# Four sums of the scan stage as accumulating transfers within SBUF, and the forget-gate product behind the B product

## The reference

```python
def step(yt, wx_t):                      # recurrence over 3136 tokens, for 64 images at once
    yt = jax.nn.sigmoid(wx_t + yt @ Vt)
    return (yt, yt)
t = t + ys                               # residual: this is x2
# third part, on xn = ln(x2)
forget_gate = sigmoid(x_ri @ Wf + bf + 2.0); input_gate = sigmoid(x_ri @ Wi + bi)
delta = softplus(x_ri @ Wd + bd) * 0.1
Bx_r = Br * x_r - Bi_ * x_i;   Bx_i = Br * x_i + Bi_ * x_r
inp = delta * input_gate * Bx
def step(h_state, _):                    # 16 steps from zero, per element
    Ah_r = Ar * h_r - Ai * h_i;   Ah_i = Ar * h_i + Ai * h_r
    return ((fg_r * Ah_r + inp_r, fg_i * Ah_i + inp_i), None)
x = x + h                                # this is x3
```

## Time and profile before

| | us |
|---|---|
| median of 3 runs | 13394.81 (13394.42 to 13395.24) |
| the profiled execution | 13372.47 |
| its span | 13370.7 |
| DVE busy | 10838.4 (81%) |
| PE busy | 10073.0 (75%) |
| ACT busy | 9336.7 (70%) |
| POOL busy | 4891.2 (37%) |
| scan stage | from about 5210 to 11715 |

### The profile page before, as it was taken

One profiled execution on the slowest core, in us unless ns is written; L12 is line 12 of the kernel. 1 busy time (PEld: TensorE's weight loads), 2 busy tenths in 40 slices (PEclk: granted clock), 3 DMA queues, 4 the chain that ended last, 5 costly groups with the idle time before them and its releaser, 6 DMA issues. The chain is left out here.

```text
span 13370.7 us, 227528 instructions
## 1 busy us (share of the span) xinstructions
PE 10073.0 (75%) x79508; PEld 7480.1 (56%) x79508; DVE 10838.4 (81%) x22723; ACT 9336.7 (70%) x21751; POOL 4891.2 (37%) x4455
## 2 busy tenths in 40 slices
PE   7888888888888886777777777777777776455544
PEld 5666666666676665555555555555555554123343
DVE  6777777777777773599999999999999999999910
ACT  6888888888888885566767667666666666467710
POOL 4444454444444442112112112112112112178856
PEclk9999999999999997777777777777777777677755
DMA  3333333333333332111121121111211211076544
GB/s 71 79 84 88 84 79 79 80 87 88 79 79 79 84 86 69 32 53 52 48 56 50 49 56 49 52 53 48 56 50 48 57 45 38 17 139 123 105 79 69
DMA packets 1599947, 907.59 MB, mean 68 GB/s; under 512 B 60693, under 2 KB 1537368, under 8 KB 1598820
## 3 DMA queue, kind: packets, MB, share of 16 engines
q1 hardware_dynamic: 1345060, 756.57, 23.7%
q10 hardware_dynamic: 207104, 102.79, 2.7%
q0 software_dynamic: 46656, 33.68, 2.0%
HBM read 567.56 MB, written 325.32 MB: 67 GB/s over the span
## 5 line engine op out<-in xcount | busy, mean ns | idle before, releaser
L1237 PEld LDWEIGHTS s_pW<-s_XU,s_vh 128*128 128x128 f32 x6272 | 1416.1, 261 | 1969.7 <-ACT s_XU L1108 1699.7
L1237 PE MATMUL s_pW<-s_XU,s_vh 128*128 128x64 f32 x6272 | 1492.9, 331 | 1071.6 <-ACT s_XU L1108 1071.6
L1108 ACT ACTIVATE s_XU<-s_pW,s_zb 128x64 f32<-128x64 f32 x3136 | 992.5, 316 | 1790.1 <-PE s_pW L1237 1739.5
L833 POOL TENSOR_TENSOR s_rst<-s_var,s_epst 128x16 f32<-128x16 f32 (+1 forms) x100 | 141.7, 1417 | 3907.2 <-DVE s_var L80 3907.2
L1266 PE MATMUL s_pG<-s_wg,s_XNT 128*128 128x384 f32 (+1 forms) x3200 | 1507.3, 560 | 37.6 <-ACT s_Z L1087 37.6
L409 ACT ACTIVATE KB<-pV,qkb 32x392 f32<-32x392 f32 x2048 | 1189.6, 581 | 25.9 <-PE pV L499 1.9
L249 POOL TENSOR_TENSOR SS<-SS,mx 128x784 f32<-128x784 f32 x512 | 769.5, 1503 | 805.0 <-DVE mx L342 804.8
L1204 PEld LDWEIGHTS s_pY<-s_hident,s_XU 128*128 128x128 f32 (+1 forms) x3200 | 751.7, 305 | 177.7 <-issue 129.5
L257 POOL TENSOR_TENSOR XR<-XR,pbias 112x512 f32<-112x512 f32 x448 | 571.8, 1276 | 648.7 <-DMA XR<-in_x_dram 648.7
L461 ACT ACTIVATE XH<-XR,nm,rs 112x128 f32<-112x128 f32 x1792 | 731.3, 482 | 90.4 <-POOL nm L268 81.8
L507 PE MATMUL pS<-KB,QT 128*64 128x196 f32 x8192 | 793.2, 336 | 0.0
(11 more groups left out here) (262 smaller groups left out, 29675.0 us busy)
## 6 DMA issues: line engine op xcount, KB each, us to landing
XL<-in_x_dram SPq DMA_DIRECT2D x64, 1568.0 KB, 12.4
XR<-in_x_dram SPq DMA_DIRECT2D x64, 1568.0 KB, 18.0
x_dram<-XR SPq DMA_DIRECT2D x64, 1568.0 KB, 8.1
xh_dram<-XH SPq DMA_DIRECT2D x64, 1568.0 KB, 8.1
e_X<-out_dram SPq DMA_DIRECT2D x64, 1568.0 KB, 15.0
s_XQ<-xh_dram ACTq DMA_DIRECT2D x384, 256.0 KB, 2.8
out_dram<-s_IN SPq DMA_DIRECT2D x96, 1024.0 KB, 5.9
e_W<-in_w_dram SPq DMA_DIRECT2D x128, 256.0 KB, 3.2
```

Source lines behind the costliest of these rows:

```text
L1108: act.activation(XU[j % 2][:, t, :], pW[t // R % 2][:, B * (t % R):B * (t % R) + B], ACT.Tanh, bias=zb[:, 0:1], scale=0.5).then_inc(u_sb, 1)
L1237: pe.matmul(pW[t // R % 2][:, B * (t % R):B * (t % R) + B], vh[:], before, start=False, stop=True, skip_group_check=True).then_inc(z_ps, 1)
```

## The change

Four additions are taken from DVE and done by DMAs that POOL issues with `accum_op=ALU.add`, which add one SBUF tile of 1 MB onto another: the two halves of the B product (`Dl` onto `BX`), the two halves of the A product (now `Z` onto `Wv`), and the last two sums (`XN` onto `X2`, then `Wv` onto `X2`). SP stores x3 from `X2` in place of `IN`, and the next load of that buffer waits for the store. The last two products are four operations of half the size, two into `XN` and two into `Wv`. The factor 0.5 and its offset move into the copy of x2, which becomes an activation with a bias of 0.5. The forget-gate product moves behind the B product and three further operations, to place 12 of the chain, and ACT's first gate waits for that.

```diff
-                    sp.wait_ge(dv, o * NV + NV)
-                    sp.dma_start(tokens(x3_d, OS * s_, OS, c),
-                                 IN[0:size(c)].rearrange("t r b c -> t (r b c)").rearrange("t (b c) -> t b c", b=OS)
-                                 ).then_inc(x3_st, 16)
+                    sp.wait_ge(both_added, (o + 1) * 16)
+                    sp.dma_start(tokens(x3_d, OS * s_, OS, c), X2[o % NX][0:size(c)]).then_inc(x3_st, 16)
...
+            def add_state(o):
+
+                n = size(o // NO)
+                pool.wait_ge(dv, o * NV + NV - 2)
+                pool.dma_start(X2[o % NX][0:n].rearrange("t b c -> t (b c)"), XN[0:n].rearrange("t b c -> t (b c)"),
+                               accum_op=ALU.add).then_inc(first_added, 16)
+
+            def add_input(o):
+
+                n = size(o // NO)
+                pool.wait_ge(dv, o * NV + NV)
+                pool.wait_ge(first_added, (o + 1) * 16)
+                pool.dma_start(X2[o % NX][0:n].rearrange("t b c -> t (b c)"),
+                               Wv[0:n].rearrange("t r b c -> t (r b c)"),
+                               accum_op=ALU.add).then_inc(both_added, 16)
...
+                    pool.wait_ge(wp_d, o + 1)
+                    pool.dma_start(Wv[0:tm].rearrange("t r b c -> t (r b c)"), Z[0:tm].rearrange("t r b c -> t (r b c)"),
+                                   accum_op=ALU.add).then_inc(wv_d, 16)
...
+                    pool.wait_ge(bp, oc + 1)
+                    pool.dma_start(BX[0:tc].rearrange("t r b c -> t (r b c)"), Dl[0:tc].rearrange("t r b c -> t (r b c)"),
+                                   accum_op=ALU.add).then_inc(bx_d, 16)
...
-                dve.wait_ge(part_sem, n + 1)
-                dve.tensor_tensor(flat(out[0:tc]), flat(out[0:tc]), flat(Dl[0:tc]), ALU.add).then_inc(sem_, 1)
...
                     after(7)
-                    turned_by(tm, Wv, inp, a, wp_d, wv_d, o)
+                    wait(dve, both_added, o * 16)
+                    turned_by(tm, Wv, Z, inp, a, wp_d)
                     dve.wait_ge(am, o * NA + 3)
                     did(dve.scalar_tensor_tensor(t1, d0, -2.0, t1, ALU.mult, ALU.subtract))
-                    dve.wait_ge(wv_d, o + 1)
-                    did(dve.scalar_tensor_tensor(flat(wv), flat(tf), 1.0, flat(wv), ALU.add, ALU.mult))
...
+                    wait(dve, first_added, o * 16)
                     did(dve.scalar_tensor_tensor(f1[:, 1], t1, -1.0, d1, ALU.add, ALU.mult))
                     did(dve.scalar_tensor_tensor(f0[:, 0], f0[:, 0], -0.25, d0, ALU.add, ALU.add))
+                    dve.wait_ge(wv_d, (o + 1) * 16)
+                    did(dve.scalar_tensor_tensor(flat(wv), flat(tf), 1.0, flat(wv), ALU.add, ALU.mult))
...
-                act.copy(X2[oc % NX][0:tc, Q * q:Q * q + Q, :].rearrange("t b c -> t (b c)"), pY[0:tc, :]).then_inc(x2_d, 1)
+                act.activation(X2[oc % NX][0:tc, Q * q:Q * q + Q, :].rearrange("t b c -> t (b c)"), pY[0:tc, :], ACT.Identity,
+                               bias=cols[0:tc, 1:2]).then_inc(x2_d, 1)
...
                 if i == 0:
-                    wait(act, dv, (oc - 1) * NV + 9)
+                    wait(act, dv, (oc - 1) * NV + 12)
```

More of the change, by code:

```diff
@@ L780, in load_x1 @@
                 c, s = divmod(o, NO)
-                wait(sp, dv, (o - NX + 1) * NV)
+                wait(sp, x3_st, (o - NX + 1) * 16)
                 sp.dma_start(X2[o % NX][0:size(c)], tokens(x1_d, OS * s, OS, c)).then_inc(x2_ld[o % NX], 16)
@@ L814, in _ @@
             pool.tensor_tensor(fld[4], fld[3], nhalf[:, 0:C], ALU.pow).then_inc(pch, 1)
+            def add_state(o):
[10 more added lines that the diff above has]
+                               accum_op=ALU.add).then_inc(both_added, 16)
             for j, s, oc, o, scan, prep in slots():
+                if o is not None and o >= 1:
+                    add_input(o - 1)
                 if scan and s == NO - 2:
@@ L819, in _ @@
                     pool.wait_ge(raw_d, j + 1)
-                    wait(pool, bx_d, (j - 1) * NO)
+                    wait(pool, bp, (j - 1) * NO)
                     pb = par_b[j % 2][0:tj]
@@ L842, in _ @@
                     pool.tensor_tensor(sa[0:tj], sa[0:tj], phalf[0:tj], ALU.pow).then_inc(mag_d, 1)
+                if oc is not None:
+                    tc = size(oc // NO)
+                    pool.wait_ge(bp, oc + 1)
+                    pool.dma_start(BX[0:tc].rearrange("t r b c -> t (r b c)"), Dl[0:tc].rearrange("t r b c -> t (r b c)"),
+                                   accum_op=ALU.add).then_inc(bx_d, 16)
+                if o is not None:
+                    add_state(o)
+            add_input(NGR - 1)
         @block.vector
@@ L898, in rows, with turned_by @@
                 return v.rearrange("t r b c -> t r (b c)")
-            def turned_by(tc, out, of, coef, part_sem, sem_, n):
+            def turned_by(tc, out, part, of, coef, part_sem):
                 def by(first):
@@ L1038, in _ @@
                     after(20)
-                    did(dve.scalar_tensor_tensor(rows(wv), both(f0[:, 0]), 1.0, rows(wv), ALU.add, ALU.mult))
-                    did(dve.scalar_tensor_tensor(rows(inp), both(f0[:, 1]), 1.0, rows(inp), ALU.add, ALU.mult))
+                    for r in range(2):
+                        did(dve.scalar_tensor_tensor(XN[0:tm, :, HC * r:HC * r + HC], f0[:, 0], 1.0, wv[:, r],
+                                                     ALU.add, ALU.mult))
                     after(22)
[L1042 to L1046, removed]
+                    for r in range(2):
+                        did(dve.scalar_tensor_tensor(grouped(wv)[:, :, HC * r:HC * r + HC], f0[:, 1], 1.0, inp[:, r],
+                                                     ALU.add, ALU.mult))
                 if scan and s == NO - 2:
@@ L1119, in _ @@
                             act.wait_ge(rs_d, oc + 1)
-                            wait(act, dv, (oc - 1) * NV)
-                            wait(act, bx_d, oc)
+                            wait(act, first_added, (oc - 1) * 16)
+                            wait(act, bp, oc)
                             wait(act, n_ps, oc * NQ)
@@ L1152, in _ @@
                         if conv:
-                            act.wait_ge(bx_d, oc + 1)
+                            act.wait_ge(bp, oc + 1)
+                        wait(act, first_added, o * 16)
                         act.activation(f1[:, 0], t1, ACT.Square, bias=cols[0:tm, 2:3]).then_inc(am, 1)
                     if o is not None and k == 22:
-                        needs(11)
+                        needs(10)
                         act.wait_ge(am, o * NA + 6)
```

18 lines of the change are left out of this document (10 added, 8 removed).

## The result

The changed kernel takes 13,694.4 us in the median of 4 runs (13,690.1 to 13,718.9), the kernel before 13,394.6: 2.3% slower, ratio 1.0230 (95% interval 1.0215 to 1.0245). The prediction was 13,825 us, slower. Its profiled execution took 13,718.9 us (span 13,717.1), 24.5 us above its median.

The account below looks back on a forecast made before the run. The ACT and PE chain, not DVE alone, was taken to set the pace. Chunks give +443 us, the thinning end -28, the last transfers +18: +433 on 13,372.5, plus 22.3 for the median, rounded to 13,825 us; range 13,580 to 14,180.

Parts of the forecast that it names:

- The gate wait: At ACT's first gate of each slot: ACT waits 5.05 us for the forget-gate product, now behind the B product.
- 5.05 - 1.0 + 1.0, about 5.0 us per slot: Behind the first gate: the wait, less 1.0 us made up by PE working ahead, plus 1.0 for PE's lower clock.
- X: Reference point in each slot: the end of ACT's fourth normalise group, from which the prediction counts its times.
- The residual: Residual copies on ACT: Identity with bias takes 683 ns against 577, four times per slot, 0.45 us on the chain.
- The slot with s = 0: Slot where ACT waited 5.95 us for POOL's `s_nmr`: hides part of the loss, so it costs 2.9 us.
- Per chunk: Chunk of four slots: 3 x 5.45 + 2.9 = 19.25 us slower, over 23 chunks +443 us.
- -28 + 18: End of the scan: some eight thinning slots win 28 us; two chained transfers ahead of the last store cost 18.
- D: Time of a 1 MB accumulate within SBUF, taken as 10 us; costed at nothing while under 12.8.
- rival 2: Accumulates are late from D = 12.8, DVE then ACT wait; at D = 14 340 us more, 14,170 us; chance 0.13.
- this rival's 13,735: Rival 1: PE's clock holds through the pause at the gate, 1.0 us less per slot, -92 us; chance 0.15.
- A made-up half (3): Rival 3: half of the gate wait is made up, 2.5 us net per slot, 13,600 us; chance 0.12.
- Rival 4: DVE is the bound; its freed 9.2 us remove POOL's 5.95 us wait per chunk: -106 us, 13,290 us; chance 0.07.

Follow-up runs that it names:

- e1: The changed kernel with only the forget-gate product put back ahead of the B product, the four accumulating transfers kept: 13,380 us.
- e3: The kernel before with only the forget-gate product moved behind the B product and three halves, all four sums still on DVE: 14,056 us.
- e5: The changed kernel with four extra matmuls on PE behind the third gate matmul of each slot, where PE else stands still: 13,658 us.
- e9: The changed kernel with the forget-gate product directly behind the B product, ahead of the three halves: 13,358 us.
- e4: The kernel before with only the residual's COPY turned into Identity with a bias of 1/2: 13,468 us.
- e2: As e1, and the residual is a COPY again without a bias, which leaves out the constant 1/2: 13,338 us.
- e6: The changed kernel with the residual a COPY again and the 1/2 added to the attention stage's projection bias: 13,677 us.
- e10: The changed kernel with each of the two adds into X2 issued as two transfers in pieces of 256 bytes: 13,952 us.
- e7: As e2, with the constant 1/2 kept by adding it to the attention stage's projection bias: 13,343 us.
- e8: As e7, with six extra matmuls on PE at the start of each slot (warm start): 13,304 us.
- e11: As e8, with one more extra matmul on PE behind each of the steps 1 to 10 of a slot: 13,300 us.

## Why the prediction was right, and what was mis-sized

1. **The gate wait.** 5.05 us forecast, 5.06 found, in every slot and with DVE as its releaser. e1 and e3 show the move behind it as the cause of the loss: it costs 661 us on before and 314 us on the kernel with the transfers, whose time without it is 13,380.
2. **What is made up, and the clock.** This is the step that failed in size: "5.05 - 1.0 + 1.0, about 5.0 us per slot". Both parts exist. The first gate starts 5.17 us later behind X than in e1 (X + 10.36, X + 5.19). From there to the slot's Exp it takes 25.9 us in e1, 24.2 in after and 23.7 in e5, where the clock holds (means of all slots from 6000 to 11000). So about 2.2 us are made up and not 1.0, and the clock takes 0.5 of it back and not 1.0 (0.4 by e5's time); with 0.2 us more from Exp to X, that is 5.17 - 2.2 + 0.5 + 0.2 = 3.7 us per slot in place of 5.0. I had counted only PE's step and gate matmul ahead; e9 shows 1.5 us of ACT's waits for PE taken over one for one. On before only 0.3 us were made up (25.1 us to the Exp, 24.8 in e3). PE's mean granted clock behind the gate fell there from 0.98 to 0.89, and from 0.96 to 0.94 between e1 and after, which may be a part of it; no run separates that.
3. **The residual.** 683 ns forecast, 682 found. Its price is not its length: 72 us on before (e4), 42 between e1 and e2, 17 in after (e6), against 0.45 x 4 x 23 = 41 in the sum.
4. **The slot with s = 0.** The `s_nmr` wait was to shrink from 5.95 to 3.4 us and is 3.26.
5. **Per chunk** 19.25 us forecast, 14.7 found; 4.55 x 23 = 105 us of the 131 us by which the forecast is high. The end came to -24 us in place of -28 + 18: 6 of these 14 us are the two transfers ahead of the last store, which took 7 us each and not 10; the other 8 are not located.
6. **The transfers.** D is 6.9 to 7.7 us in the median, under the 10 taken and above the 4.4 us of the estimate that the prediction gives beside it, so rival 2 had no case. Its room at D = 10, given as 7 us, is 8.3 us by the prediction's own deadline (38.3 less 30). e10 shows that the deadline of the A product was about right (31 less 21.3 is 9.7 us of lateness, 9.5 found) and that lateness is not the only price.
7. **Rivals.** The clock did not hold (1), and had it held, the price was some 36 us and not 92 (e5); that the time lies nearest to this rival's 13,735 is chance. A made-up half (3) was too much; the net 1.4 us (5.06 less 3.7) lie between it and the forecast. Rival 4 is the gain that the transfers bring: 88 us from e4 to e1, 52 from before to e7. The wait at the gate took it back several times over.
8. **The level.** The expert stage's 1655.6 us in the profiled execution was 15 to 27 us under all later ones, which fits the 22 us that I added for the median. Yet after's profiled execution lies above its median, by 24.5 us. These 47 us between the two ways of counting and the 37 us of the later first store and the longer expert stage, neither of them forecast, nearly cancel: there the forecast was lucky.

## What to carry to other kernels

Work taken off a busy engine is worth what the wait at its end was worth, here 6 us per chunk at most; and an instruction moved later on it is charged to whoever needs its buffer next, even when the engine itself gained more (DVE's busy time fell by 865 us, the kernel lost 300 us). Before moving one, add up from the trace what will stand between the last point that the waiting engine itself releases and the moved instruction's end, and compare that with the time at which the waiter arrives: e9 and after differ in three operations of 1.14 us, and in 337 us. A short wait (1.5 us in e9) can be free where the waiter would wait for a slower partner anyway; e3, where next to nothing was made up, shows that it can't be counted on.

## What the runs showed of the hardware that was not expected

- A 1 MB accumulating transfer within SBUF, in rows of 8 KB, lands in 6.9 to 7.7 us in the median, against 5.8 us for a 1 MB store, and POOL issues it in about 0.9 us beside a busy DVE (after). The few of 512 KB, with half as many rows, took 7.3 to 7.4 us, no less. Two of 512 KB in pieces of 256 bytes, issued together, land in 11.6 to 12.4 us each and hold POOL for 2.1 us each (e10).
- With the adds in pieces of 256 bytes, the 256 KB loads on another queue land in 6.2 us in place of 3.2 in the median (e10 against after).
- With 0.11 us more per residual PE's clock rose later in a slot that holds no residual, and that slot was 1.5 us longer (e4). Raising the mean clock of the stage from 0.76 to 0.83 and 0.86 brought 39 and 44 us (e8, e11).
